# A graph layer's gather: the bound on the index taken from its indirect loads, and the table lengthened to every index of 14 bits

## The reference, cut to what matters

```
deg  = segment_sum(ew_sl, row_sl)            # edges and self loops
norm = dinv[row] * ew * dinv[col]            # dinv = rsqrt(deg)
h7   = segment_sum((xn @ W)[col] * norm, row) + b
gcn  = relu(h7 @ W1 + b1) @ W2 + b2
mix  = (linear attention: k, v normalised by head, q @ (k^T v) / N, gelu MLP)
x    = x + gcn + mix
x    = x + moe(layernorm(x))                 # 8 experts, top 2, hidden 512
```

## Time and profile before

| | |
|---|---|
| median of 3 runs | 4129.89 us (4127.36 to 4131.44) |
| span of the profiled execution, first to last instruction | 4123.7 us |
| time of that execution apart from its span | not given by the page |
| instructions | 75106 |
| TensorE (PE) busy | 3332.8 us, 81% |
| VectorE (DVE) busy | 2916.4 us, 71% |
| ScalarE (ACT) busy | 1436.5 us, 35% |
| GpSimd (POOL) busy | 2805.8 us, 68% |
| the gather's loads (L1638) on POOL | 1664, from 1013.2 to 3187.8 us |
| mean TensorE clock granted | 0.901 |

### The profile page before, as it was taken

How to read it: one execution, slowest core, us unless ns; L and a number is a source line. 1 busy time by engine, 2 the same in 40 slices (tenths; PEclk the granted TensorE clock), 3 DMA queues, 4 the chain that set the end, 5 groups by cost and what they waited for, 6 DMA issues and landing times. The chain is left out here.

```text
span 4123.7 us, 75106 instructions
## 1 busy us (share of the span) xinstructions
PE 3332.8 (81%) x20075; PEld 2428.2 (59%) x20075; DVE 2916.4 (71%) x7656; ACT 1436.5 (35%) x4413; POOL 2805.8 (68%) x2528
## 2 busy tenths in 40 slices
PE   7677777444888888888888888888888499999995
PEld 6455455343444444444445666666666489999985
DVE  8899999785666676666656666666666855555587
ACT  3355555353111111111102333333333345555552
POOL 0388888663777777777777777777777056666663
PEclk9688877655999999999968999999999799999998
DMA  2111111386444444444434555545544322222367
GB/s 82 18 3 3 3 3 3 66 273 208 122 126 126 126 125 126 123 125 126 129 101 124 151 151 151 151 151 151 151 149 147 103 64 70 70 71 70 120 243 265
DMA packets 283329, 471.48 MB, mean 114 GB/s; under 512 B 94311, under 2 KB 180076, under 8 KB 283247
## 3 DMA queue, kind: packets, MB, share of 16 engines
q0 software_dynamic: 139776, 272.64, 25.0%
q1 hardware_dynamic: 131423, 189.44, 13.5%
q10 hardware_dynamic: 12050, 8.45, 0.6%
HBM read 349.06 MB, written 122.65 MB: 114 GB/s over the span
## 5 line engine op out<-in xcount | busy, mean ns | idle before, releaser
L1638 POOL DMA_INDIRECT rows<-table,idx x1664 | 1668.6, 1003 | 507.9 <-issue 418.5
L2086 PE MATMUL ps_seg<-rows,pick 128*128 128x256 f32 x3328 | 1054.8, 422 | 346.8 <-DMA rows<-table,idx 337.2
L1921 DVE TENSOR_TENSOR acc<-acc,ps_seg 128x256 f32 x1664 | 697.8, 419 | 609.3 <-PE ps_seg L2086 497.6
L2086 PEld LDWEIGHTS ps_seg<-rows,pick 128*128 128x128 f32 x3328 | 569.6, 195 | 755.5 <-DMA rows<-table,idx 643.4
L771 POOL DMA_INDIRECT records<-sort_rec,sort_addr x280 | 527.5, 1884 | 258.4 <-DVE sort_rec L874 155.5
L1763 DVE TENSOR_SCALAR pick<-iota_row,loc,ewt 128x128 f32<-128x128 f32 x1680 | 520.2, 361 | 3.9
L2548 POOL DMA_INDIRECT y_rows<-arena,spot x204 | 276.7, 1356 | 213.9 <-DVE idx L2603 142.2
L2690 PE MATMUL ps_h<-arena,up_now 128*128 128x128 f32 x3264 | 401.3, 276 | 4.1 <-DVE up_now L2618 2.1
L926 PE MATMUL ps_out<-acc 128*128 128x240 bf16 x1568 | 280.2, 363 | 145.1 <-DVE acc L860 144.9
L2690 PEld LDWEIGHTS ps_h<-arena,up_now 128*128 128x128 f32 x3264 | 382.5, 193 | 7.4 <-issue 7.3
L2674 PE MATMUL ps_y<-down_now,arena 128*128 128x256 f32 x1632 | 385.9, 379 | 0.0
(11 more groups left out here) (396 smaller groups left out, 4833.6 us busy)
## 6 DMA issues: line engine op xcount, KB each, us to landing
rows<-table,idx POOLq DMA_INDIRECT x1664, 2.8
acc<-y_rows SPq DMA_DIRECT2D x20, 896.0 KB
xn<-xn_dram SPq DMA_DIRECT2D x100, 128.0 KB, 2.1
xT_dram<-xT SPq DMA_DIRECT2D x98, 128.0 KB
xn<-xT_dram SPq DMA_DIRECT2D x49, 256.0 KB, 3.5
skip<-skip_dram SPq DMA_DIRECT2D x49, 256.0 KB, 3.9
x_rows<-acc SPq DMA_DIRECT2D x49, 256.0 KB, 2.6
ffn_rows<-kv SPq DMA_DIRECT2D x49, 256.0 KB, 2.3
```

Source lines behind the costliest of these rows:

```text
L1638: pool.indirect_dma_start(out=rows[:, t, :], out_offset=None, in_=k.table, in_offset=bass.IndirectOffsetOnAxis(idx[:, h, t:t + 1], 0), bou ...
L1921: dve.tensor_tensor(here, here, sums(u), ALU.add).then_inc(added[u], 1)
L2086: last = pe.matmul(sums(t), pick[:, h, t, :], rows[:, t, :], start=True, stop=True)
```

## The change

The indirect loads of `gather_step` carry no bound any more, and the register that held it goes. `k.table` gets 16384 rows in place of 12544, one for every value of the 14 bits. The 3840 rows behind the nodes are set to zero in the setup by five stores of 768 rows each from the same zero tile, put between the stores over the record arrays and the one over the padding of `xn_dram`; the setup's last wait counts them. `table_blocks` is taken from the first 12544 rows. Nothing else is changed; the indirect DMAs of the sort and of the experts keep their bounds.

```diff
--- before.py
+++ after.py
@@ -39,6 +39,8 @@
 FIRST_PAIR = 56
 assert all(STEP_TILES * min(FIRST_PAIR + i, STEPS) * BLOCKS >= 2 * (i + 1) * TILES_USED for i in range(PAIRS))
 DST_BITS = 14
+SPARE = 6
+assert ((1 << DST_BITS) - NODES) % (SPARE * P) == 0 and NODES < 1 << DST_BITS and SPARE * D <= TILES
 GRANULE_BITS = 3
 GRANULE = 1 << GRANULE_BITS
 LOT = 28
@@ -136,7 +138,7 @@
         k.place_dram = nc.dram_tensor("place_dram", [2, LOTS, BLOCKS], BF16).ap()
         k.places_dram = nc.dram_tensor("places_dram", [STEPS, STEP_TILES], I32).ap()
         k.xn_dram = nc.dram_tensor("xn_dram", [NODES + AHEAD * P, D], F32).ap()
-        k.table = nc.dram_tensor("table", [NODES, D], F32).ap()
+        k.table = nc.dram_tensor("table", [1 << DST_BITS, D], F32).ap()
         k.skip_dram = nc.dram_tensor("skip_dram", [NODES, D], F32).ap()
         k.xT_dram = nc.dram_tensor("xT_dram", [NODES, D], F32).ap()
         k.ffn_rows = nc.dram_tensor("ffn_rows", [NODES, D], F32).ap()
@@ -358,6 +360,9 @@
                     for half in range(2):
                         sp.dma_start(k.records[r].rearrange("(p t) w -> p (t w)", p=P)[:, half * TILES:(half + 1) * TILES],
                                      zero).then_inc(zeroed, 16)
+                spare = zero[:, 0:SPARE * D].rearrange("p (t d) -> p t d", d=D)
+                for at in range(NODES, 1 << DST_BITS, SPARE * P):
+                    sp.dma_start(k.table[at:at + SPARE * P, :].rearrange("(t p) d -> p t d", p=P), spare).then_inc(zeroed, 16)
                 pad = zero[:, 0:AHEAD * D].rearrange("p (t d) -> p t d", d=D)
                 sp.dma_start(k.xn_dram[NODES:, :].rearrange("(t p) d -> p t d", p=P), pad).then_inc(zeroed, 16)
 
@@ -374,7 +379,7 @@
                 sp.dma_start(k.places[:, :], k.places_dram.rearrange("(o b) t -> o (b t)", o=1)).then_inc(places_in, 16)
                 sp.wait_ge(places_in, 16)
                 sp.wait_ge(place_in, 16)
-                sp.wait_ge(zeroed, 80)
+                sp.wait_ge(zeroed, 80 + 16 * len(range(NODES, 1 << DST_BITS, SPARE * P)))
 
             @block.scalar
             def _(act):
@@ -1021,7 +1026,7 @@
         x_blocks = A["x"].rearrange("(t p) d -> p t d", p=P)
         xn_blocks = k.xn_dram.rearrange("(t p) d -> p t d", p=P)
         skip_blocks = k.skip_dram.rearrange("(p t) d -> p t d", p=P)
-        table_blocks = k.table.rearrange("(t p) d -> p t d", p=P)
+        table_blocks = k.table[0:NODES, :].rearrange("(t p) d -> p t d", p=P)
 
         turns = [(w, g) for g in range(0, TRIPS, 4) for w in range(2)]
         span = lambda g: range(g, min(g + 4, TRIPS))
@@ -1626,7 +1631,6 @@
                 for h in range(HEADS_PER_CHUNK):
                     part_of = slice(h * HEADC, (h + 1) * HEADC)
                     pool.memset(headmask[part_of, part_of], 1.0 / N_NODES).then_inc(mask_made, 1)
-                last_node = pool.to_reg(NODES - 1)
 
                 def gather_step(n, h):
                     pool.wait_ge(idx_done, n + 1)
@@ -1637,8 +1641,7 @@
                             pool.sem_inc(gather_held, 1)
                         pool.indirect_dma_start(
                             out=rows[:, t, :], out_offset=None, in_=k.table,
-                            in_offset=bass.IndirectOffsetOnAxis(idx[:, h, t:t + 1], 0),
-                            bounds_check=last_node, oob_is_err=False).then_inc(got[t], 16)
+                            in_offset=bass.IndirectOffsetOnAxis(idx[:, h, t:t + 1], 0)).then_inc(got[t], 16)
 
                 for h in range(2):
                     gather_step(h, h)
```

## The result

The changed kernel takes 4053.26 us (median of 4, 4052.49 to 4061.0) against 4129.28 us (4127.36 to 4131.44) beside it: ratio 0.9818, 95% interval 0.9804 to 0.9832. That is 76 us less. The forecast was 33 us less, 4097 us: the right way, by less than half the size.

A forecast was written before the change was run, and what follows sets the result against it. POOL, issuing 1664 gathers one after another, was taken to set the gather stage's length. Saving 1664 x 20 ns = 33 us, with setup and other terms at 0, gave 4129.9 - 33 = 4097 us; range 3990 to 4145 us.

The forecast's parts named there:

- What bounds the kernel: Gather stage, 1013 to 3192 us: POOL sets its length, 1664 x (1.003 + 0.305) = 2177 us.
- Setup at nothing: Setup: five more stores cost 0, covered by counting of blocks on DVE and PE; uncovered, 11 to 33 us.
- Rows fetched, landing, pause: Altered gathers: same rows fetched, landing stays 2.8 us, pause stays 0.30 us.
- The price of the bound: Altered gathers: dropping the bound saves 20 ns each, 1664 x 20 ns = 33 us.
- Fact (4): Indirect DMAs: adding to the target costs 4.4 ns an index; a gather's 998 ns are 7.8 ns an index.
- fact (2): Sort's scatters: one with most indices refused takes 1.55 us like one with none; a refused index costs the same.
- the case of a small gain: Altered gathers: 5 to 60 ns less each, 8 to 100 us in all, chance 0.38.
- Nothing is late next: Gather stage: DVE (0.87 us per gather) and PE (at most 1.16 us) stay below a period of 1.29 us.
- The sign it gave for TensorE taking over: Gather stage shrinks by less than 1664 times the period's change, and POOL's waits on PE exceed 0.3 us.
- No change: Altered gathers: the test is made anyway or hidden, time stays 4130 us; chance 0.37.
- The large gain: Altered gathers: bound handled index by index; 100 ns each would save 166 us, giving 3964 us; chance 0.11.
- Slower by another form: Altered gathers: form without a bound takes a dearer path on POOL, 30 ns more each, 4180 us; chance 0.14.

The follow-up runs named there:

- e9: Kernel before with half of the segment sum left out on TensorE and VectorE, bound kept: 4131.21 us.
- e10: Changed kernel with half of the segment sum left out on TensorE and VectorE: 4050.76 us.
- e16: Changed kernel with the bound taken from the experts' gathers too: 4051.55 us, 0.9807 of the kernel before.
- e1: Kernel before with the bound alone removed, table left at 12544 rows: ratio 1.0017 to the kernel before, which took 4427.24 us beside it.
- e4: Changed kernel with VectorE's scaling of keys and values in two halves: ratio 1.0020 to the kernel before, 4427.24 us beside it.
- e6: Bound alone removed from the kernel before, repeated on another chip: ratio 1.0017 to the kernel before, 4460.98 us beside it.
- e8: Changed kernel with VectorE's scaling in two halves, repeated on another chip: ratio 1.0009 to the kernel before, 4460.98 us beside it.
- e14: Kernel before with the long table and the stores of zeros alone, bound kept: 4128.45 us, 0.9998 of the kernel before.
- e5: Layer replaced by loops of 12 indirect DMAs per form, alone on POOL: 128 indices took 998 ns with a bound, 942 without.
- The split: Kernel before without the bound, VectorE's scaling of keys and values in two halves: 4038.52 us, 0.9781 of the kernel before; bound alone removed, 4054.75 us.
- e3: The changed kernel itself, run again: ratio 1.0021 to the kernel before, which took 4427.24 us beside it.
- e12: The changed kernel itself, run once more: 4051.57 us, with the kernel before at 4128.22 us beside it.
- e2: Kernel before with the long table and stores of zeros, bound kept: ratio 1.0002 to the kernel before, 4427.24 us beside it.

## Why the prediction was wrong in size

- **What bounds the kernel: right.** POOL, gather after gather. 1664 x (0.958 + 0.305) us = 2102 us is the stage after, and halving the other engines' share of the segment sum moved nothing (e9, e10). It held in the kernels of the result and of e9 to e16; in e1 to e4 and e6 to e8 POOL did not set the pace, which nothing in the trace before could show.
- **Setup at nothing: right, by the cover named.** The transfers' part of it was fair, all done by 47 us; the issue was not: 5.8 us were forecast for the five stores, 18.45 us shown, three times as much, so they stand between 12 and 31 us and not between 12 and 19. SP had 102 us to spare, and e14 shows no cost.
- **Rows fetched, landing, pause: right.** Landing 2.8 us, pause 0.30 us, with the bound and without; no part of its price lies in the pause.
- **The price of the bound: the step that failed.** "Between 0 and 190 ns I take 20 ns" should have been 52 ns (56 alone). 52 x 1664 = 86.5 us. The working behind it had two faults. Fact (4) divided 998 ns by 128 and read 7.8 ns an index, "mostly of that kind of work"; e5 gives about 1 ns an index and some 870 ns for the transfer. From an index's price it then argued that a test can only be small, but the test's cost is also mostly a transfer's: 35 to 39 ns at 64 and 32 indices, 56 at 128. And fact (2), one time for any mixture of good and refused indices, is true (e5: 998 ns again) but says only that the outcome of the test costs nothing, not that the test is cheap. Nothing in the trace of before gave the fixed part: every indirect DMA there has 128 indices. It could not have been read, only bounded, and the value should have been put nearer the middle of what the case of a small gain held (5 to 60 ns). That case, held likeliest by 0.38 against 0.37, did hold the 52 ns, and the range held the time; with nothing in the rows to set the size, the sign was close to an even bet and the 20 ns a guess.
- **"Nothing is late next": right for the engines, but something was given back.** Of 86.5 us, 75.1 came: the excess of the long gathers grew by 11.4 us (8.7 to 20.1), 8.9 of them at VectorE's scaling and 2.4 at the picks. With the shorter beat 60 gathers began during a scaling where 20 had; what the beat would meet could not be read ahead. The prediction saw the longest duration of 1438 ns in the earlier trace rows and did not ask what made it. The split shows what it was. The sign it gave for TensorE taking over (a stage that shrinks by less than 1664 times the change of the period) would have misled anyone who took the period by its median: no pause of POOL exceeded 0.35 us.
- **The rules of the Trainium skill.** The Trainium skill's page "DMA: Bandwidth & Descriptors" calls the generation of descriptors small and variable (section "Anatomy of one DMA"). e5 agrees in one way: 96 more indices cost 94 ns. But a fixed part, by the estimate above about 870 ns on POOL, stands beside it, so in this stage of 1664 transfers POOL is the limit, and each step that is dropped from the fixed part counts. That software computes these descriptors, as the Trainium skill says in the section "SWDGE vs HWDGE vs iDMA" of the same page, gave the right sign; no run here shows what that software does.
- **The rivals.** No change: right only for the runs in which POOL had lost the pace (e1, e3), for another reason than was given. The large gain: out, no index-by-index price of that size. Slower by another form: out; the experts' gather is 50 ns shorter without its bound too.

## What to carry to other kernels

Where the rows show one engine issuing without slack, look for options to take off the instruction that it repeats, and count in nanoseconds times repeats; a bound that no index can reach is such an option, if the data guarantee it. A duration divided by the number of elements is no price per element until the same form has been seen at two sizes. And the same saving off the pacing engine is worth nothing, so look first at who waits for whom. Last, a small excess in the pacing instruction is worth a look of its own: the split of another engine's instruction gave 16 us here, a fifth of what the bound gave.

## What the runs showed of the hardware that I had not expected

- An indirect load with a bound takes 904 ns of POOL for 32 rows, 938 for 64 and 998 for 128 (e5), by these an estimated 870 ns plus 1 ns an index, and 0.305 us of pause behind it. So four gathers of 32 rows cost POOL 3.6 us where one of 128 costs 1.0.
- A bound costs a load of 128 rows 52 to 56 ns of POOL, one of 64 or 32 rows 35 to 39, and a scatter of 128 rows 13; as register or as constant alike (998 ns).
- A gather that begins while VectorE runs the 128 x 512 float32 product of two SBUF operands (685 ns) lasts longer by what is left of it less 0.13 us; the 128 x 128 picks (341 ns, TENSOR_SCALAR) delay some gathers too, but the reduction of 128 x 512 (679 ns) and the adds with an operand in PSUM delay none of the 557 that begin during them. Cut in two, the product shows as two records of 420 ns that overlap, 756 ns together, 72 ns more of VectorE each time, and the kernel is still faster.
- On one chip the kernel before took 4427 us beside e1 to e4 and 4128 us beside e9 to e12. The stages around the gather stage hardly differ (the gathers begin near 1014 us in either, and 945 to 950 us against 933 to 936 follow them), so nearly all of it lies in the gather stage, where the granted clock was 0.85 in e2 and e3 against 0.96 in the kernel before at its other pace. A low clock alone does not make the slow pace: e9 had 0.81 there, though with half of the sums, and kept POOL's beat. What does, the runs don't tell.
